# Routed experts' up product: weights and tokens split into a high part and a remainder in every block, three single-pass products in place of a native one

## The reference, cut to what matters

```python
x = x + xattn(ctx, layernorm(x), ...)          # a state space scan over 512 steps
h = layernorm(x)                               # 4 x 512 tokens of 512 numbers
aff = sigmoid(h @ wa)                          # 16 experts, each token takes 2
def expert(h, g, gb, w1, b1, w2, b2):          # D = 512, F = 256
    y = gelu(h @ g + gb) * (h @ w1 + b1)
    return y @ w2 + b2
x = x + sum_of_two_shared_experts(h) + weighted_sum_of_two_routed_experts(h)
```

## Time and profile before

| | |
|---|---|
| time, median of 3 runs | 992.35 us (988.01 to 993.58) |
| the profiled execution | 990.75 us, its span 989.0 us |
| PE, DVE, ACT, POOL busy over the span | 83%, 64%, 52%, 56% |
| PE matmul L1559 (up product) | 376 rows, 592 ns each |
| PE matmul L1576 (down product) | 188 rows, 594 ns each |
| granted clock of PE over the span | 0.933 |

### The profile page before, as it was taken

The page is one execution under the profiler, slowest core; times in us unless marked ns, Lnnn a source line. Parts: engine busy times, 40 slices in busy tenths (PEclk is TensorE's granted clock), DMA queues, the critical chain, the costliest instruction groups (busy, mean ns, idle before and its releaser), DMA issues.

```text
span 989.0 us, 14660 instructions
## 1 busy us (share of the span) xinstructions
PE 820.5 (83%) x4030; PEld 562.8 (57%) x4031; DVE 636.4 (64%) x669; ACT 512.0 (52%) x831; POOL 554.4 (56%) x483
## 2 busy tenths in 40 slices
PE   6987487677777777777588998989999999999991
PEld 2323476666666766666566776777445444544440
DVE  4858899989999998898877675542223332333230
ACT  3578498778888897898124321201233333333330
POOL 2211199889999899999555244020344444444331
PEclk9966699989999898998799998989999999999996
DMA  5010031112132112110311112046867877787533
GB/s 157 0 48 1 25 104 43 43 43 60 49 106 65 58 50 84 45 44 1 115 50 49 43 38 81 12 168 270 288 153 200 209 181 208 205 233 157 86 43 42
DMA packets 32421, 95.40 MB, mean 96 GB/s; under 512 B 5088, under 2 KB 5216, under 8 KB 29040
## 3 DMA queue, kind: packets, MB, share of 16 engines
q1 hardware_dynamic: 20400, 65.37, 19.4%
q0 software_dynamic: 11968, 29.37, 14.8%
HBM read 122.11 MB, written 21.36 MB: 145 GB/s over the span
## 4 chain that ended last, share of the span: by engine, by line
PE 59%; DVE 18%; issue 8%; POOL 7%; ACT 4%; DMA 2%; DVEq 0%; SPq 0%; POOLq 0%; ACTq 0%
PE ps L1559 16%; DVE r L953 11%; PE ps L1576 8%; POOL r L464 6%; PE ps L1364 5%; PE ps L1341 5%; PE ps L1418 5%; PE ps L1420 4%; PE ps L1419 4%; PE ps L1273 3%; PE ps L1550 2%; DVE r L962 2%; PE ps L1281 2%; PE ps L1296 1%; ACT mem L687 1%
## 5 line engine op out<-in xcount | busy, mean ns | idle before, releaser
L953 DVE TENSOR_TENSOR_SCAN r<-r,ps 128x1024 f32<-128x1024 f32 x128 | 286.0, 2271 | 24.2 <-PE ps L1364 15.5
L464 POOL TENSOR_TENSOR r<-r,mem 128x512 f32<-128x512 f32 x224 | 288.6, 1318 | 12.2 <-DVE r L953 6.8
L1341 PE MATMUL ps<-ident,mem 128*128 128x128 f32 x1024 | 145.5, 289 | 74.3 <-DVE r L953 56.7
L675 ACT ACTIVATE r<-mem,nega 128x511 f32<-128x511 f32 x256 | 168.7, 713 | 37.6 <-DVE r L953 37.6
L1341 PEld LDWEIGHTS ps<-ident,mem 128*128 128x128 f32 x1024 | 119.6, 148 | 97.5 <-issue 80.7
L1559 PE MATMUL ps<-r,mem 128*128 x376 | 169.1, 592 | 0.4 <-ACT mem L816 0.4
L1364 PE MATMUL ps<-ident,r 128*128 128x128 f32 x1024 | 145.3, 283 | 16.9 <-DVE r L962 10.4
L560 POOL DMA_INDIRECT out<-sg,ids x47 | 74.5, 1586 | 144.2 <-DMA out<-sg,ids 113.4
L1364 PEld LDWEIGHTS ps<-ident,r 128*128 128x128 f32 x1024 | 120.6, 145 | 25.1 <-DVE r L962 13.6
L687 ACT ACTIVATE mem<-mem,bc 128x512 f32<-128x512 f32 x192 | 124.7, 712 | 14.0 <-PE ps L1341 13.1
L1559 PEld LDWEIGHTS ps<-r,mem 128*128 128x128 f32 x376 | 71.2, 190 | 89.1 <-issue 89.1
(11 more groups left out here) (172 smaller groups left out, 1000.8 us busy)
## 6 DMA issues: line engine op xcount, KB each, us to landing
r<-in_r_up SPq DMA_DIRECT2D x47, 1024.0 KB
mem<-in_r_down SPq DMA_DIRECT2D x47, 512.0 KB
mem<-cm_rows SPq DMA_DIRECT2D x64, 256.0 KB, 3.3
mem<-in_r_b SPq DMA_DIRECT2D x4, 2048.0 KB, 11.7
r<-in_x SPq DMA_DIRECT2D x4, 1024.0 KB, 4.9
xn_scratch<-r SPq DMA_DIRECT2D x16, 256.0 KB, 2.3
out<-acc POOLq DMA_DIRECT2D x16, 256.0 KB, 2.7
mem<-in_ctx_t SPq DMA_DIRECT2D x4, 512.0 KB, 8.3
```

What stands on the lines that cost most here:

```text
L464: pool.tensor_tensor(state[:, k % 2, ec], state[:, k % 2, ec], cb[:, k % CROWS], ALU.mult).then_inc(s["weighed_p"], 1)
L675: act.activation(decay[:, k % 2, ec, 1:L], delta[:, b, ec, 1:L], ACT.Exp, scale=nega[:, ec, n:n + 1]).then_inc(s["decay_ready"], 1)
L953: dve.tensor_tensor_scan(state[:, half, ec:ec + 2].rearrange("p e l -> p (e l)"), decay[:, half, ec:ec + 2].rearrange("p e l -> p (e l)"), ...
L1341: mm = pe.transpose(ps[:, ec, lt * P:(lt + 1) * P], dbu_t[:, k % 2, lt, ec * P:(ec + 1) * P], ident[:])
```

## The change

In every routed block the up weights of the block's expert and its tokens are split. ACT copies the weights in two parts of 128x1024 to `up_head` (`weight_head`), and its copy of the tokens becomes a rounding copy. DVE subtracts: `weight_rest` (two parts of 128x1024) and `token_rest` (128x512). PE's up product is twelve single-pass products instead of four native ones. The heads and remainders have two buffers (`r % 2`), laid over `acc`, which holds the shared experts' rows until they are stored; hence the waits for `early_stored` and `late_stored`. Weights are split two blocks ahead. ACT turns tokens two blocks ahead instead of three, ahead of the gelu. SP's load of up weights waits for the remainders of the slot's last block instead of its product.

```diff
+        up_head = view(acc_again, 0, 2, 2 * UP)[:, :, 0:UP]
+        up_rest = view(acc_again, 0, 2, 2 * UP)[:, :, UP:2 * UP]
+        xgt_rest = view(blk_val_again, 0, 2, D)
...
             def load_up(j, r):
                 if not isinstance(j, int) or j >= SLOTS:
-                    wait_apart(sp, s["h_ready"], j - SLOTS + 1)
+                    wait_apart(sp, s["upr_made"], 2 * (j - SLOTS + 1))
...
             def turn_tokens(j, half):
                 act.wait_ge(s["xgt_ready"], j + 1)
                 since(act, s["h_ready"], j - 1)
-                act.copy(xgt[:, half], ps[:, 4 + half]).then_inc(s["xgt_copied"], 1)
+                act.copy(one_pass(xgt[:, half]), ps[:, 4 + half]).then_inc(s["xgt_copied"], 1)
+
+            def weight_head(j, r, round_, part):
+
+                if part == 0:
+                    act.wait_ge(s[f"up_{r}"], 16 * (round_ + 1))
+                    since(act, s["h_ready"], j - 1)
+                slot_j = act.value_load(blk_slot[0:1, ds(j, 1)], min_val=0, max_val=SLOTS - 1)
+                act.copy(one_pass(up_head[:, r % 2, up_half(part)]), up_half_of(slot_j, part)).then_inc(s["uph_made"], 1)
...
+                more = not isinstance(j, int) or j + 2 < NBLK
+                if more:
+                    weight_head(j + 2, (r + 2) % RING, round_ + (r + 2) // RING, 0)
+                    turn_tokens(j + 2, r % 2)
                 hidden_gate(j, r % 2)
+                if more:
+                    weight_head(j + 2, (r + 2) % RING, round_ + (r + 2) // RING, 1)
                 if not isinstance(j, int) or j >= 2:
                     block_result(j - 2, r % 2, (RING // 2) * round_ + (r - 2) // 2)
                 turn_hidden(j, r % 2)
-                if not isinstance(j, int) or j + 3 < NBLK:
-                    turn_tokens(j + 3, (r + 1) % 2)
-
+
+            act.wait_ge(s["blocks_ready"], 3)
+            act.wait_ge(s["early_stored"], 16 * NT // 2)
+            weight_head(0, 0, 0, 0)
+            weight_head(0, 0, 0, 1)
             act.wait_ge(s["so_ready"], NT)
             turn_tokens(0, 0)
             turn_tokens(1, 1)
-            turn_tokens(2, 0)
+            act.wait_ge(s["late_stored"], 16 * NT // 2)
+            weight_head(1, 1, 0, 0)
+            weight_head(1, 1, 0, 1)
...
+            def weight_rest(j, half, part):
+
+                slot_j = dve.value_load(blk_slot[0:1, ds(j, 1)], min_val=0, max_val=SLOTS - 1)
+                dve.wait_ge(s["uph_made"], 2 * j + part + 1)
+                dve.tensor_tensor(one_pass(up_rest[:, half, up_half(part)]), up_half_of(slot_j, part),
+                                  up_head[:, half, up_half(part)], ALU.subtract).then_inc(s["upr_made"], 1)
+
+            def token_rest(j, half):
+                dve.wait_ge(s["xgt_copied"], j + 1)
+                dve.tensor_tensor(one_pass(xgt_rest[:, half]), ps[:, 4 + half], xgt[:, half],
+                                  ALU.subtract).then_inc(s["xgr_made"], 1)
...
                 hidden_bias(j, r % 2)
+                if not isinstance(j, int) or 0 < j < NBLK - 1:
+                    token_rest(j + 1, (r + 1) % 2)
+                if more:
+                    weight_rest(j + 2, r % 2, 0)
                 hidden(j, r % 2)
                 if not isinstance(j, int) or j >= 2:
                     add_bias(j - 2, r % 2)
-
+                if more:
+                    weight_rest(j + 2, r % 2, 1)
+
+            weight_rest(0, 0, 0)
+            weight_rest(0, 0, 1)
+            add_shared(3, every)
+            token_rest(0, 0)
+            token_rest(1, 1)
+            weight_rest(1, 1, 0)
+            weight_rest(1, 1, 1)
...
+            def up(j, r):
+                pe.wait_ge(s["xgr_made"], j + 1)
                 since(pe, s["hb_ready"], j - 1)
-                for kc in range(KC):
-                    mm = pe.matmul(ps[:, r % 2], xgt[:, r % 2, kc * P:(kc + 1) * P], up_weights(slot_j, kc),
-                                   start=(kc == 0), stop=(kc == KC - 1))
+                for part in range(2):
+                    pe.wait_ge(s["upr_made"], 2 * j + part + 1)
+                    kcs = range(part * KC // 2, (part + 1) * KC // 2)
+                    mm = split_product(ps[:, r % 2], [(xgt[:, r % 2, kc * P:(kc + 1) * P], xgt_rest[:, r % 2, kc * P:(kc + 1) * P],
+                                                       up_head[:, r % 2, kc * 2 * F:(kc + 1) * 2 * F],
+                                                       up_rest[:, r % 2, kc * 2 * F:(kc + 1) * 2 * F]) for kc in kcs],
+                                       first=(part == 0), last=(part == 1))
                 mm.then_inc(s["h_ready"], 1)
```

More of the change, by code:

```diff
@@ L163, in bass_xattn_scan_moe_kernel @@
         b2_all = view(mem, B2_AT, E, D)
-        xgt = view(mem, LATE_AT, 2, D)
+        xgt = view(split, LATE_AT, 2, D)
         hyt = view(mem, LATE_AT + 4 * D, 2, F)
@@ L219, in bass_xattn_scan_moe_kernel @@
         row_hot = view(r0, 8192, 2, GROUP, P)
-        blk_val = sb("blk_val", [P, 2, GROUP, 2 * NBLK])
+        with ExitStack() as listing:
+            blk_val = listing.enter_context(nc.sbuf_tensor("blk_val", [P, 2, GROUP, 2 * NBLK], F32))
+        blk_val_again = sb("blk_val_again", [P, 2 * GROUP * 2 * NBLK])
         half_i = sb("half_i", [P, 2 * ((NBLK + 3) // 2)], I32)
@@ L267, in bass_xattn_scan_moe_kernel @@
         sh_ready sg_ready sy_ready syh_made syr_made wh_made wr_made wah_made war_made xr_made scores_ready scores_copied logits_copied so_ready so_added
-        up_0 up_1 up_2 up_3 down_0 down_1 down_2 down_3 xg_0 xg_1 xg_2 xg_3 xgt_ready xgt_copied h_ready
+        uph_made upr_made xgr_made up_0 up_1 up_2 up_3 down_0 down_1 down_2 down_3 xg_0 xg_1 xg_2 xg_3 xgt_ready xgt_copied h_ready
         hb_ready hg_ready hy_ready hyt_ready hyt_copied o_ready yb_ready y_ready y_even y_odd
@@ L286, in wait_apart, with up_half, up_half_of @@
             eng.sem_inc(S["waits_passed"], 1)
-        def up_weights(slot_j, kc):
-            return up_w[:, bass.ds(slot_j, 1), kc * 2 * F:(kc + 1) * 2 * F].rearrange("p o n -> p (o n)")
+        def up_half(part):
+            return slice(part * UP // 2, (part + 1) * UP // 2)
+        def up_half_of(slot_j, part):
+            return up_w[:, bass.ds(slot_j, 1), up_half(part)].rearrange("p o n -> p (o n)")
         def down_weights(slot_j, fc):
@@ L1218, in expert_of @@
                 return dve.value_load(blk_e[0:1, ds(j, 1)], min_val=0, max_val=E - 1)
-            add_shared(3, every)
+            def weight_rest(j, half, part):
[7 more added lines that the diff above has]
+                                  ALU.subtract).then_inc(s["xgr_made"], 1)
             def hidden_bias(j, half):
@@ L1547, in turn_tokens @@
                 pe.wait_ge(s[f"xg_{r}"], 16 * (round_ + 1))
-                since(pe, s["xgt_copied"], j - 1)
+                since(pe, s["xgr_made"], j - 1)
                 for kc in range(KC):
@@ L1551, in turn_tokens @@
                 mm.then_inc(s["xgt_ready"], 1)
-            def up(j, r, round_):
-                slot_j = pe.value_load(blk_slot[0:1, ds(j, 1)], min_val=0, max_val=SLOTS - 1)
-                pe.wait_ge(s["xgt_copied"], j + 1)
-                pe.wait_ge(s[f"up_{r}"], 16 * (round_ + 1))
+            def up(j, r):
+                pe.wait_ge(s["xgr_made"], j + 1)
                 since(pe, s["hb_ready"], j - 1)
-                for kc in range(KC):
-                    mm = pe.matmul(ps[:, r % 2], xgt[:, r % 2, kc * P:(kc + 1) * P], up_weights(slot_j, kc),
-                                   start=(kc == 0), stop=(kc == KC - 1))
+                for part in range(2):
[5 more added lines that the diff above has]
+                                       first=(part == 0), last=(part == 1))
                 mm.then_inc(s["h_ready"], 1)
@@ L1580, in step @@
             def step(j, round_, r):
-                up(j + 1, (r + 1) % RING, round_ + (r + 1) // RING)
+                up(j + 1, (r + 1) % RING)
                 turn_hidden(j, r)
@@ L1590, in _ @@
             turn_tokens(1, 1, 0)
-            up(0, 0, 0)
+            up(0, 0)
             turn_tokens(2, 2, 0)
@@ L1600, in _ @@
             last = NBLK - 1
-            up(last, last % RING, last // RING)
+            up(last, last % RING)
             turn_hidden(last - 1, (last - 1) % RING)
```

## The result

The changed kernel takes 1015.12 us (median of 4 runs, 1013.28 to 1019.44) against 992.97 us (988.01 to 997.44) for the kernel before in the same series: ratio 1.0231, 95% interval 1.0172 to 1.0289. It is slower, as forecast, and within the range, but by 22 us where 7.4 were worked out. The profiled execution took 1014.8 us, its span 1013.1.

The account below looks back on a forecast made before the run. PE was taken to bound the routed blocks at 5.81 us each. 31 blocks at 6.0 (+5.9), 12 unchanged and the start (+1.5) gave +7.4 us: 998.2 profiled, 1.6 more for the median, 1000 us; range 982 to 1018.

Parts of the forecast that it names:

- The sum: Whole kernel: 5.9 us over 31 blocks, 0 over the other 12, 1.5 at the start, together 7.4 us slower.
- much slower: Rival: register loads begun during subtractions run long, 6.4 us a block in the routed stage, 1019 us; chance 0.14.
- PE's term: Routed blocks on PE: up product 3.43 to 2.72 us, block 5.81 to 5.10, 31 us saved if PE stayed the bound.
- The moved wait: Up weights: ScalarE wants them two blocks earlier than PE did, at 788.8 us against a landing at about 790.6, so late.
- What is late next, as a loop over four blocks: Blocks 7 to 37: late weights return through the next hidden bias and up product; 5.9 us a block, taken as 6.0.
- Landing 5.4 us: Loop of late weights: a 1024 KB load of up weights lands in 5.4 us, taken between 4.9 and 5.9.
- PE's clock ... nothing: PE in the routed stage: granted clock 0.96 to 1.00, costing 0.2 us a block, hidden under DVE's pace.
- DVE's step 5.42 to 5.99, taken 5.8: DVE per routed block: added subtractions and exposed register loads of 0.85 to 1.04 us make it the pace, 5.8 us.
- Start 1.5 us: First routed blocks: token rest, block 1's head waiting for stored shared rows and block 2's rests add 1.5 us.
- Tail 0: End of the kernel: scatters follow one another, 4.60 us from issue to landing each, and stay unchanged.
- Interfaces shared with GpSimd: Rival: DVE's two subtractions slow down beside GpSimd, 3.4 us more a block, some 1145 us; chance 0.03.
- The faster rival: Routed stage: register loads hide (5.42 us a block), weights are there in time, about 980 us; chance 0.16.

Follow-up runs that it names:

- a_one_load: The changed kernel with one register load of the slot per block on ScalarE and one on VectorE instead of two each; 1027.39 us, ratio 1.0296.
- b_pe_only: The kernel before with twelve single-pass up products on one rounded copy of block 0's weights and rounded tokens, no splitting in the blocks; 986.46 us, ratio 0.9899.
- a_up_first: The changed kernel with SP's load of up weights of block m+2 issued ahead of down weights of block m; 998.97 us, ratio 1.0045.
- c_up3: The changed kernel with up weights issued three blocks ahead instead of two, and ahead of the down weights; ratio 1.0023.
- c_up3_gelu: The changed kernel with up weights three blocks ahead, ahead of down weights, and gelu and `hidden` ahead of the head copies and rests; ratio 1.0299.

## Why the prediction came out as it did

- **The sum.** The direction came out as forecast, for the reason given. The size did not: 22 us where 7.4 were worked out. The number came nearest to the rival "much slower" (1019 us), whose mechanism, long register loads, a_one_load speaks against. That 1015 lies within the range is in part luck: the room up there had been left for another cause, and two errors of opposite sign took something off each other (31 blocks at 6.50 us and not 6.0; the last ten at 5.40 and not 5.8).
- **PE's term: right.** Single-pass products follow at 0.23 us (741.55 on), and a block on PE is 2.7 us of up product. The 31 us are real on PE and mostly out of reach: b_pe_only's stage got 6.9.
- **The moved wait: right in kind.** Head copies wait for fresh weights, in the places foreseen (blocks 7, 10, 13), and a_up_first removes the loss by undoing it. This is why the sign held.
- **"What is late next, as a loop over four blocks": path wrong, and its terms too small.** 31 x 0.19 = 5.9 us was worked out; these 31 blocks cost 21.4 more than before. The loop that I followed went through the up product of block m, back to the down product of m-4. The one in the trace goes through `hidden`, which the prediction itself names as standing behind the rest: late weights, head, first rest, `hidden`, turn, down product, SP, landing. It measures 18.7 us over three blocks, 6.2 us a block. But the path alone doesn't make the difference: priced as in the prediction (5.4 + 5.4 + 0.85 + 1.03 + 0.1 + 1.13 + 0.42 + 0.66 + 1.88) it is 16.9 us, 5.6 a block, less than the 5.9 of the loop that I took. The rest is in what stands on it: the landing, PE's part from `hidden` to the end of the down product (3.9 us where these prices make 3.0), and the clock.
- **Landing 5.4 us: too low.** The five landings in the chain up to 880 us took 8.40, 5.26, 6.74, 6.23 and 7.18 us, 6.8 on average; around the first of them the DMA share was 0.92 (725 to 732 us). The loads of the earlier trace rows are from other stages. 1.4 us more in a loop of three blocks is 0.45 us a block.
- **"PE's clock ... nothing": wrong.** The mean was 0.94, but a mean isn't what the loop pays: right behind a stall it was 0.50, and the down product there took 3.43 instead of 1.72 us.
- **DVE's step 5.42 to 5.99, taken 5.8: over-sized.** I read 0.85 us between neighbours in the earlier trace rows as the price of a register load. The second row there had waited 0.42 us for PE: the gap was a wait. Without one, the pair takes 0.34 us, and a clean step 4.68. The pace of the last ten blocks, foretold as near 5.8, was 5.40.
- **Start 1.5 us: mis-sized, measured 8.7 to the first hidden bias and 7.9 to the fourth.** The wait for the last shared rows was named, but not priced, though the trace of the kernel before had the 9.95 us in GpSimd's wait.
- **Tail 0: measured 4.6 us.** Scatters that were behind had to follow at their own pace: from 980.74 to the last at 1002.57 are four, 5.46 us each. It doesn't come from late weights: in a_up_first and c_up3, where none are late, the tail is 21.8 and 21.3 us. The end of the chain is made of scatters:

```profile
980.74 4.58 DMA out<-sg,ids
985.36 0.74 issue
986.11 4.57 DMA out<-sg,ids
```

- **"Interfaces shared with GpSimd": no sign on DVE.** The subtraction of 1024 columns takes 1208 to 1301 ns in all kernels here, beside GpSimd's DMA issues. The Trainium skill, "GPSIMD Engine Reference", section Specifications, speaks of contention for the shared interfaces; in this stage the trace shows none in DVE's durations. GpSimd's side is told below.
- **The faster rival** (980 us) supposed that weights are there in time. With c_up3 they are, and the gain still doesn't come: 4.8 us less in the stage than before, and a start 10.9 us longer.

Still open: how the 21.4 us divide between landing, PE's part and the clock. No run took the clock's fall away alone, and none changed the landing alone.

## What to carry to other kernels

When a wait moves to another engine, write down everything that stands behind the waiting instruction there, and follow each item to the resource that releases the next load. Each gives a loop; divide its time by the blocks that it spans, and the largest quotient holds the pace. Price its transfers by a stretch with the same traffic, and its matrix products by rows right behind a stall. Before moving work off the bound engine, ask what stands just under it; here scatters (5.5 us a block), SP's two loads (2.69 us each in the earlier trace rows) and DVE (4.7 to 5.1) lay under PE's 5.81, so 31 us of savings were worth 7. A consumer that moves two blocks ahead needs its producer's issue moved ahead as well: turning round two lines on SP was worth 18 us by the runs' times, 26 by the stage of one profile.

## What the runs showed that I had not expected

- A register load is mostly hidden on DVE while the engine works: 0.34 us from a 256-column product to the next addition across one. It isn't always: at 719.14 and 724.65 the same addition came after 0.59 and 0.66 us of idle time, with no wait for another engine ahead of it. Behind a wait it shows too: 0.30 and 0.79 us (`DVEq L1246` in the chain at 734.59 and 746.62).
- A 256 KB store took 9.8 to 12.0 us to land beside a 2048 KB load and the weight loads behind it, 5.8 us with these held back, and 2.6 us in the median of the page.
- In 10 of 47 cases GpSimd's issue of a scatter took over 1.75 us, up to 2.63, with the weight rests running beside it; in the kernel before the longest was 1.64 us. Each of the ten overlaps a weight rest, but many short ones do as well, and in c_up3_gelu, with as many rests, the longest was 1.81 us. What decides was not tried.
